# Seam between the projections and the attention of a fused two-layer kernel: the last value stores issued in the attention's block, and one dummy product instead of three ahead of the first scores

## The reference, cut to what matters

```python
x = L0_attn_x
x = _layernorm(x + _L0_attn_ref(x, ...), axis=-1)   # retention, 16 heads, two halves of 256 tokens
x = _layernorm(x + _L0_ffn_ref(x, ...), axis=-1)    # ternary weights, 1024 hidden
x = _layernorm(x + _L1_attn_ref(x, ...), axis=-1)   # attention over the heads of each token
x = _layernorm(x + _L1_ffn_ref(x, ...), axis=-1)    # 8 experts, top 2, capacity 160
```

```python
kv1 = jnp.einsum('bshe,bshd->bsed', K1, V) * SCALE
kv2 = jnp.einsum('bshe,bshd->bsed', K2, V) * SCALE
w1 = jnp.einsum('bshe,bsed->bshd', Q1, kv1)
w2 = jnp.einsum('bshe,bsed->bshd', Q2, kv2)
attn = w1 - lmb * w2
```

## Time and profile before

| what | us |
|---|---|
| runs before | 896.16, 890.45, 890.84 |
| median | 890.84 |
| profiled execution, its own time | 892.54 |
| its span, first to last instruction | 890.9 |
| outside the span in that execution | 1.64 |
| PE busy, of the span | 815.3 |

### The profile page before, as it was taken

The page is one execution under the profiler, slowest core; times in us unless marked ns, Lnnn a source line. Parts: engine busy times, 40 slices in busy tenths (PEclk is TensorE's granted clock), DMA queues, the critical chain, the costliest instruction groups (busy, mean ns, idle before and its releaser), DMA issues. The chain is left out here.

```text
span 890.9 us, 23450 instructions
## 1 busy us (share of the span) xinstructions
PE 815.3 (92%) x8950; PEld 667.5 (75%) x8950; DVE 598.5 (67%) x1439; ACT 488.7 (55%) x1018; POOL 272.7 (31%) x335
## 2 busy tenths in 40 slices
PE   6999999998899999998999899998988879999960
PEld 5888888887677777766777688886655549999950
DVE  3677778778557777778555425577667886657627
ACT  2544443443777777775974244556575435454426
POOL 1257763221112222224000000124443134656344
PEclk9999999999999999999999999999999989999985
DMA  8600000000000000001478534435222314566439
GB/s 321 197 21 22 18 24 18 18 12 3 1 1 1 1 1 1 1 1 34 126 196 199 132 92 131 136 101 198 93 85 99 103 31 121 142 201 161 119 64 343
DMA packets 74637, 79.55 MB, mean 89 GB/s; under 512 B 21824, under 2 KB 65728, under 8 KB 74176
## 3 DMA queue, kind: packets, MB, share of 16 engines
q1 hardware_dynamic: 69584, 72.36, 26.6%
q0 software_dynamic: 3968, 5.25, 3.4%
q10 hardware_dynamic: 1008, 0.91, 0.3%
HBM read 50.70 MB, written 27.79 MB: 88 GB/s over the span
## 5 line engine op out<-in xcount | busy, mean ns | idle before, releaser
L729 DVE TENSOR_TENSOR r_prob<-r_pS,const 128x512 f32<-128x512 f32 x128 | 81.9, 682 | 24.7 <-PE r_pS L551 24.7
L1106 DVE SCALAR_TENSOR_TENSOR f_gl<-att_res,small_first,f_gh 128x512 fp32r<-128x512 f32 x64 | 47.3, 747 | 35.7 <-ACT f_gh L1031 33.4
L1685 POOL TENSOR_TENSOR att_res<-att_res,t_hy 128x1024 f32<-128x1024 f32 x8 | 15.5, 1958 | 165.2 <-DVEq L2182 165.2
L960 PE MATMUL f_pY<-wpjT,f_gh 128*128 128x256 f32 x256 | 65.4, 290 | 0.3 <-DVE f_gl L1106 0.3
L961 PE MATMUL f_pY<-wpjT,f_gl 128*128 128x256 f32 x256 | 62.7, 279 | 0.0
L1374 PEld LDWEIGHTS q_bank<-q_xT,att_res 128*64 128x64 f32 x1024 | 57.3, 140 | 7.2 <-issue 4.2
L1374 PE MATMUL q_bank<-q_xT,att_res 128*64 128x128 f32 x1024 | 60.9, 279 | 0.0
L960 PEld LDWEIGHTS f_pY<-wpjT,f_gh 128*128 128x128 f32 x256 | 48.1, 188 | 15.9 <-issue 13.4
L2595 POOL DMA_INDIRECT sum_dram<-e_yo,y_id x24 | 43.1, 1795 | 54.6 <-ACT e_yo L2732 39.5
L1025 ACT ACTIVATE att_res<-f_pH 128x512 f32<-128x512 f32 x64 | 38.0, 594 | 38.6 <-PE f_pH L945 37.8
L2713 ACT ACTIVATE e_hh<-e_pH 128x320 fp32r<-128x320 f32 x64 | 26.2, 433 | 54.0 <-PE e_pH L2637 53.8
(11 more groups left out here) (336 smaller groups left out, 2350.6 us busy)
## 6 DMA issues: line engine op xcount, KB each, us to landing
kv_dram<-att_res SPq DMA_DIRECT2D x32, 256.0 KB, 3.5
t_ring<-kv_dram SPq DMA_DIRECT2D x128, 64.0 KB, 2.3
wi<-L_ffn_wi SPq DMA_DIRECT2D x8, 1024.0 KB, 5.0
wo<-L_ffn_wo SPq DMA_DIRECT2D x8, 1024.0 KB, 7.6
x_res<-L_attn_x SPq DMA_DIRECT2D x8, 512.0 KB, 7.0
q_dram<-att_res SPq DMA_DIRECT2D x16, 256.0 KB, 3.5
t_q<-q_dram SPq DMA_DIRECT2D x8, 512.0 KB, 4.4
x_dram<-x_res SPq DMA_DIRECT2D x8, 512.0 KB, 3.0
```

The costliest lines, as they stand in the source:

```text
L729: dve.tensor_tensor(prob[t % 2][:, r, :, :], pS[r][:, :, :], dec[:, r, :, :], ALU.mult)\
L960: pe.matmul(out, gh[c % 4][:, cols], net.wpjT[:, c, :], start=(c == 0 and t % 2 == 0), stop=False, skip_group_check=True)
L1106: dve.scalar_tensor_tensor(out=gl[c % 4][:, :], in0=g[c][:, :], scalar=net.lnw[:, c:c + 1], in1=gh[c % 4][:, :], op0=ALU.mult, op1=ALU.sub ...
```

## The change

The two stores of the values of the last batch are left out of the first block's SP stream (the loop runs over n = 0, 1 for the last batch) and stand instead as the first instructions of SP in the second block, with no wait in front of them other than the barrier. `keep_turning` ahead of the scores runs once instead of three times. Nothing else is changed.

```diff
+    def keep_tokens(sp, b, n):
+
+        tokens = net.kv_dram[n - 1, :, b * SEQ * RUN:(b + 1) * SEQ * RUN].rearrange("r (j h c) -> h r j c", j=KD, h=2)
+        for h in two:
+            sp.dma_start(tokens[h], res[b % 2][n][h * ROWS4:(h + 1) * ROWS4, :, :]).then_inc(stored[n][b % 2].sem, 16)
+
+    net.keep_last_values = lambda sp: keep_tokens(sp, BATCH - 1, 2)
+
     def sync(sp):
         for b in range(BATCH):
-            for n in range(3):
+            for n in range(3 if b < BATCH - 1 else 2):
                 sp.wait_ge(item_ready.sem, item_ready.after(ITEMS * b + KD * (n + 1)))
...
                 else:
-                    tokens = net.kv_dram[n - 1, :, b * SEQ * RUN:(b + 1) * SEQ * RUN].rearrange("r (j h c) -> h r j c", j=KD, h=2)
-                    for h in two:
-                        sp.dma_start(tokens[h], res[b % 2][n][h * ROWS4:(h + 1) * ROWS4, :, :]).then_inc(kept, 16)
+                    keep_tokens(sp, b, n)
...
     @block.sync
     def _(sp):
+        net.keep_last_values(sp)
         for m in range(1, CHUNKS):
...
-        keep_turning(pe, bank(pT[:, :, :]), net.table["ones"], 3)
+        keep_turning(pe, bank(pT[:, :, :]), net.table["ones"], 1)
         for n in range(ALL + 3):
```

## The result

The changed kernel took 890.57 us in the median of 20 runs (887.2 to 894.3). The kernel before, in 20 runs that include the three of the prediction, took 894.47 us (890.45 to 896.16). The ratio is 0.9955, 95% interval 0.9943 to 0.9967: about 4.0 us, within 1%. The means differ by 3.46 us (894.00 and 890.54). The prediction had a gain of 4.94 us, a ratio of 0.9945, and a time of 885.9 with a range up to 889.6. So the ratio lies inside the interval, close to its end, while the time is 4.7 us off and outside the range.

A forecast was written before the change was run, and what follows sets the result against it. PE was taken to bound the attention, with SP's drain and the dummies holding back its start at the seam. 1.65 + 3.08 + 0.21 = 4.94 us off 890.84 gave 885.9 us, range 883.2 to 889.6.

The forecast's parts named there:

- The base: Whole kernel: the summed gain is taken from 890.84 us, the median of the runs shown, giving 885.9.
- the dummies' term: Seam ahead of the first scores: four of six dummy records go, removing 3.08 us.
- the moved stores cost nothing: Head of SP's second block: two issues of some 0.6 us each, hidden by the later wait for scores; cost 0.
- The barrier: Seam between the blocks: without the last value stores SP is ready earlier, DVE is last, barrier 1.65 us earlier.
- the first scores' clock: First scores behind the seam: they run at full instead of half clock, a gain of 0.21 us.
- Full clock after the change: Seam and first scores: PE idles 1.06 us instead of 2.69, so the granted clock stays at full throughout.
- Rival A: Seam: the clock falls in spite of the shorter gap, upon the scores; gain 3.05 us, time 887.8; chance 0.14.
- All of it reaches the end: From seam to end: the whole 4.94 us arrives, since engines start anew behind the barrier and PE has no slack.
- Rival D: Later, above all in the routing: the shift changes where the clock falls, adding or taking 1 to 3 us; chance 0.09.
- B: Seam: the barrier comes no earlier, for instance because its wait hides an instruction load; gain 3.3 us, 887.5; chance 0.06.
- C: Attention: without the three dummies the clock stays at half; slower than before, 899.9 us at 28 us of it; chance 0.03.

## Why the prediction was right and wrong

Two steps failed. The base put the time outside the range, and the dummies' term was too large; both are taken up below. A third, that the moved stores cost nothing, is in doubt.

**The barrier: right.** SP was last by its two value stores, DVE came next. 1.65 us was predicted; the idle time ahead of PE went from 2.69 to 1.07 or 1.06 in every trace with the stores moved and a dummy ahead, by 1.63. The two parts add: where the clock holds, the seam is 5.43 us before, 3.71 with the dummies alone, 3.80 with the stores alone and 2.09 with both, and 1.72 + 1.63 = 3.35 is 5.43 - 2.09. At the seam the moved stores cost nothing: with them alone it is 5.43 - 3.80 = 1.63 us shorter, the whole of the barrier. Further back this isn't shown, because of the wait in the attention. One detail was off: SP issues them from 506.7 to 507.9, not from 505.7; what it does in the microsecond behind the barrier the rows don't show. In the trace shown nothing waits for it: SP's wait for the scores of steps 0 to 3 still lasts 5.1 us behind the stores.

**The dummies: a term that was mis-sized.** The prediction removed 3.08 us of dummies and added 0.21 for the first scores' clock, 3.29 together. Of this 1.72 is there in every trace, the two products at full clock with what stands between; the remaining 1.57 is the fall of the clock, which two of the four traces of the kernel before don't have (6.84 and 6.90 less 5.43 are 1.4 and 1.5, and in the first trace 0.2 more is the first score's). By these four the mean seam is (6.84 + 5.43 + 5.44 + 6.90) / 4 = 6.15, and the gain 6.15 - 2.09 = 4.1, where 4.94 was summed. The means of the runs show 3.5. The prediction took the fall in its one trace for a property of the gap: it compared busy shares ahead of falls and asked only whether the changed kernel would have one, never whether the old one always had.

**Full clock after the change: right.** The idle time of 1.06 us brought no fall in any of the six traces that have it, and 1.75 us in neither of two. Rival A did not come.

**All of it reaches the end: not shown.** In the first trace of the changed kernel the attention lay 4.93 us earlier at its third step and 5.14 at its end, and what its span lacks is 1.69 at the MLP and 0.87 in the norm. In its other two traces the ninth step comes 0.8 and 0.9 us late, so there the attention itself gives a part back. From the first score to the end of the span it is 379.3, 379.0, 379.3 and 380.3 us in the four traces of the kernel before, and 381.6, 381.3 and 381.4 in the three of the changed one, 2.0 more in the mean. Of this, 1.3 is the MLP (a mean excess of 1.61 against 0.33); the rest is mostly the wait in the attention and that in the norm, which is 0.8 to 0.9 us in two of the eight traces with the stores moved and 0.15 to 0.2 in two more. None of the three is in every trace with the stores moved: the kernel without a dummy has 379.0. The fall at the MLP also occurs without the change. But three of three against one of four at the MLP leaves it open whether the changed kernel has it more often, and the other two waits are in no trace without the moved stores. If all of it belonged to the change, the gain would be about 4.1 - 2.0 = 2.1; the measured 3.5 lies between this and the 4.1 above. So how much of the missing part is the kernel before, which doesn't always have the fall at the seam, and how much the changed kernel gives back, was not settled.

**The base and the range: the step that put the time outside.** The sum was taken from the median of three runs with the reason that the edit doesn't touch what makes the runs differ. The profiled execution of the same kernel stood 1.7 above it, and the prediction noted that the three spread by 5.3 upward. Over 20 runs the median is 894.47: 890.45 and 890.84, two of the first three, are among the three fastest of the twenty, which was luck. The reason was wrong as well. One thing in which executions of the kernel before differ is the fall upon the dummies, worth 1.4 to 1.6 us, and the edit touches it: the forecast took it off, in full, from a median that need not have held it. A larger difference lies ahead of the seam: the last projection record ends anywhere from 504.74 to 508.44 in the four traces. What the fast runs had, no trace shows. With the median of twenty the same sum gives 889.5, and the range moved with it, 886.8 to 893.2, holds the measured 890.57. Rival D named a right mechanism, a clock fall elsewhere, but for the routing, and from the same base. The fall came at the MLP; from the second half of its first `down` to the first step of the closing norm, with the routing between, it is 243.5 to 244.1 us in all seven traces of the two kernels, so the routing took nothing back.

**B and C: didn't come.** The barrier moved by what was summed, so nothing else was holding it; the clock was never down in the attention with the change.

## What to carry to other kernels

A barrier is left when the last engine's drain ends (SP's at 507.17 here and POOL's event at 507.2; with the change DVE's and POOL's event at 505.5), so work that nobody needs soon, such as a store, can be moved behind it when its issuer is last; read the drains, not only the compute rows, and then follow the loads of the same issuer, whose slack can be small (0.4 us for the ninth step's keys). Of a clock fall seen in one trace, take several traces of the same kernel before counting it as gained or lost, and give a time as a ratio to a base of enough runs. A dummy product belongs into idle time that another engine sets, where it delayed nothing in three traces; ahead of work that is ready, it costs its full length, 0.86 us each here at full clock.

## What the runs showed of the hardware

One program gives different traces with respect to the clock. With the same 2.69 us of idle time and the same work ahead of it, the clock fell to its half in two of five traces and held in three. There are falls ahead of the seam, too, where the traces already differ: the last projection record ended at 504.74, 508.44, 508.38 and 506.24 us in the four traces of the kernel before. In the second and third of them the clock was at 0.91 from 220 to 260 us, in the fourth from 240 to 260, where the first has 1.00; the first has 0.91 from 400 to 420 instead. How much of the 3.7 us between them comes from that wasn't worked out. The rows of the second:

```profile
220.00:240.00 20.00, 16.84 (x134) 12.27 (x124) 9.28 (x27) 11.20 (x23) 2.79 (x8) 0.91 0.01 2
240.00:260.00 20.00, 17.80 (x112) 12.68 (x112) 13.10 (x29) 13.90 (x24) 3.86 (x8) 0.91 0.00 1
400.00:420.00 20.00, 16.66 (x149) 12.15 (x150) 16.40 (x48) 8.01 (x14) 7.18 (x12) 1.00 0.00 1
```

SP's drain took 368 ns behind an issued DMA in both kernels, whichever stores stood in front of it, and 7 ns at the two other block ends of the first trace of each.
